# Position scores of an attention stage made evenly over the tiles, 14 tiles ahead

## The reference, cut to what matters

```python
x = L0_attn_w                                     # (2, 2048, 256) float32
x = x + 0.5 * ffn(layernorm(x))                   # 8 experts of rank 16, top 2
x = x + attn(layernorm(x))
x = x + 0.5 * ffn(layernorm(x))

def attn(w):                                      # 16 heads of width 16, 2 sequences
    AC = einsum('bhid,bhjd->bhij', q + u_bias, k)
    BD = einsum('bhid,hjd->bhij', q + v_bias, rp) # rp: (4095 relative positions) @ Wr.T
    BD = rel_shift(BD)                            # row i is moved by i
    return softmax((AC + BD) * 0.25) @ v
```

## Time and profile before

| | us |
|---|---|
| median of 3 runs | 3423.48 (3422.01 to 3426.68) |
| the profiled execution | 3423.38, its span 3421.6 |
| busy in the span: TensorE | 3015.8 (88%) |
| ScalarE | 2591.6 (76%) |
| VectorE | 2486.6 (73%) |
| POOL | 2404.1 (70%) |
| mean granted clock of TensorE | 0.944 |

### The profile page before, as it was taken

One profiled execution on the slowest core, in us unless ns is written; L12 is line 12 of the kernel. 1 busy time (PEld: TensorE's weight loads), 2 busy tenths in 40 slices (PEclk: granted clock), 3 DMA queues, 4 the chain that ended last, 5 costly groups with the idle time before them and its releaser, 6 DMA issues. The chain is left out here.

```text
span 3421.6 us, 112672 instructions
## 1 busy us (share of the span) xinstructions
PE 3015.8 (88%) x40768; PEld 2061.1 (60%) x40768; DVE 2486.6 (73%) x4784; ACT 2591.6 (76%) x4106; POOL 2404.1 (70%) x4104
## 2 busy tenths in 40 slices
PE   4556399999999999998999999999999999989965
PEld 2444066666666666666666666666666666666645
DVE  2555177777787878787878787877787787878866
ACT  2334388888888878787888888887888888878832
POOL 3223687777788878786878877877877887868820
PEclk8778599999999999999999999999999999999987
DMA  5232799999999999999999989999999999999951
GB/s 188 92 104 97 185 202 208 201 201 204 199 210 208 212 198 211 199 212 191 207 217 208 216 198 205 208 205 198 215 206 207 208 210 211 206 198 206 209 155 50
DMA packets 326603, 655.70 MB, mean 192 GB/s; under 512 B 191536, under 2 KB 283568, under 8 KB 292784
## 3 DMA queue, kind: packets, MB, share of 16 engines
q0 software_dynamic: 190464, 524.79, 72.4%
q1 hardware_dynamic: 135600, 123.75, 14.8%
HBM read 77.48 MB, written 46.14 MB: 36 GB/s over the span
## 5 line engine op out<-in xcount | busy, mean ns | idle before, releaser
L653 POOL DMA_DIRECT2D score<-score x3968 | 2272.5, 576 | 632.8 <-ACT score L894 568.9
L892 ACT COPY score<-pos_bank 128x512 f32<-128x512 f32 x2048 | 1087.9, 608 | 439.1 <-PE pos_bank L768 434.3
L902 ACT ACTIVATE score<-score,low 128x1024 f32<-128x1024 f32 x1024 | 1211.3, 1184 | 17.5 <-DVE low L953 11.7
L835 PE MATMUL pt_bank<-ident_sb,score 128*128 128x128 f32 x8192 | 1121.5, 278 | 29.5 <-issue 20.6
L835 PEld LDWEIGHTS pt_bank<-ident_sb,score 128*128 128x128 f32 x8192 | 954.5, 142 | 317.3 <-DVE prob_t L962 78.7
L953 DVE CUSTOM_DVE_ANT_0 score<-ac_bank,score 128x1024 f32<-128x1024 f32 x512 | 627.0, 1225 | 571.0 <-PE ac_bank L821 526.2
L962 DVE COPY prob_t<-pt_bank 128x512 f32<-128x512 f32 x1536 | 1008.6, 684 | 10.0 <-PE pt_bank L835 9.1
L953 DVE CUSTOM_DVE_ANT_0 score<-ac_bank,score,low 128x1024 f32<-128x1024 f32 x512 | 656.5, 1282 | 115.4 <-PE ac_bank L821 95.9
L768 PE MATMUL pos_bank<-pos,qv 96*32 96x512 bf16 (+15 forms) x12160 | 635.6, 318 | 80.8 <-DMA qv<-qv_parts 53.8
L849 PE MATMUL acc_bank<-prob_t,vs 128*32 128x128 f32 x16384 | 678.2, 281 | 29.8 <-issue 29.5
L821 PE MATMUL ac_bank<-ks,qu 96*128 96x512 bf16 x2048 | 628.8, 389 | 13.0 <-issue 7.1
(11 more groups left out here) (94 smaller groups left out, 935.9 us busy)
## 6 DMA issues: line engine op xcount, KB each, us to landing
score<-score POOLq DMA_DIRECT2D x3968, 129.0 KB, 6.5
pos<-pos_parts SPq DMA_DIRECT2D x96, 128.0 KB, 9.3
ks<-k_parts SPq DMA_DIRECT2D x192, 64.0 KB, 7.5
qu<-qu_parts SPq DMA_DIRECT2D x768, 16.0 KB, 7.8
qv<-qv_parts SPq DMA_DIRECT2D x576, 16.5 KB, 6.9
v_heads<-v_sb SPq DMA_DIRECT2D x8, 1024.0 KB, 7.3
vs<-v_heads SPq DMA_DIRECT2D x32, 256.0 KB, 9.0
pos_parts<-part SPq DMA_DIRECT2D x16, 384.0 KB, 2.7
```

The source lines that it names most:

```text
L653: pool.dma_start(pairs_of_tiles(score[s::QUAD, at:at + FT, :], 0), pairs_of_tiles(score[s::QUAD, at:at + FT, :], QUAD - 1 - s))\
L835: last = pe.matmul(PT[c % 2][:, t * P:(t + 1) * P], lhsT=score[:, slot(k), c * BANK + t * P:c * BANK + (t + 1) * P], rhs=ident_sb[:, :], i ...
L892: act.copy(score[:, at + f, c * BANK:(c + 1) * BANK], ring(m)[:, :]).then_inc(pos_out, 1)
L902: act.activation(cols, cols, ACT.Exp, bias=low[:, slot(k), NH - 1:NH], scale=-1.0)\
```

## The change

Three things change together, and the counts of the waits with them.
- The 17 items of a group are spread as 4, 4, 4 and 5 over its four tiles (`MADE_OF`), and `made_at` picks them by (k + POS_AHEAD) % 4, so that each body makes the items of the tile k + POS_AHEAD, two in each half (2 and 3 for the last of a group).
- `POS_AHEAD` is 14 in place of 11. The items of a group are thus made at k % 4 = 2, 3, 0, 1. Before the first content 14 tiles of positions are made, not 12. ScalarE's take of a tile waits for the slot's old tile alone to be turned (two bodies before), not for its whole group.
- `FOLD_AT` is 4 (bank 1), and the fold is made at k % 4 = 2, `finish` at k % 4 = 3, each one tile later. The load of `qv` is issued at k % 4 = 1, and five groups of it stand ahead of the loop.

```diff
--- before.py
+++ after.py
@@ -539,7 +539,7 @@
             NT = 12 * NI
             FIRST, STEPS = 4, 2
             PAIR = NB * NI
-            POS_AHEAD, AC_AHEAD = 11, 2
+            POS_AHEAD, AC_AHEAD = 14, 2
             GQ = FT * P
             QVW = GQ + 16
             PSL = 4
@@ -617,8 +617,8 @@
             def slot(k):
                 return k % (RING * FT)
 
-            MADE_AT = (range(0), range(0, 6), range(6, 12), range(12, ITEMS))
-            FOLD_AT = MADE_AT[1].stop
+            MADE_OF = (range(0, 4), range(4, 8), range(8, 12), range(12, ITEMS))
+            FOLD_AT = MADE_OF[0].stop
             ACT_COPIES = ((1, 3), (), (3,), (3,))
             COPIES = [(k, c) for k in range(FT) for c in range(NK)]
             BY_ACT = [(k, c) for k, c in COPIES if c in ACT_COPIES[k]]
@@ -626,7 +626,7 @@
 
             def fold_no(k):
 
-                return (k - FT - 1) // FT
+                return (k - FT - 2) // FT
 
             def ring(m):
 
@@ -634,7 +634,7 @@
 
             def made_at(k, h):
 
-                items = MADE_AT[k % FT]
+                items = MADE_OF[(k + POS_AHEAD) % FT]
                 middle = (items.start + items.stop) // 2
                 return range(items.start, middle) if h == 0 else range(middle, items.stop)
 
@@ -710,7 +710,7 @@
 
                 def body(step, k):
                     j = (k + POS_AHEAD + 5) // FT
-                    if k % FT == 0 and group_there(step, j):
+                    if k % FT == 1 and group_there(step, j):
                         positions_made(step, k + POS_AHEAD)
                         load_qv(step, j)
                     pair = k // PAIR + 1
@@ -746,7 +746,7 @@
                 load_vs(0, 0)
                 load_qu(0, 1)
                 load_ks(0, 1, range(len(K_PARTS)))
-                for j in (2, 3):
+                for j in (2, 3, 4):
                     positions_made(0, FT * (j - 1) - 1)
                     load_qv(0, j)
                 tile_steps(sp, body, 4)
@@ -864,19 +864,19 @@
                         if there(step, n):
                             for m in made_at(k, h):
                                 positions(step, n // FT, m)
-                        if h and k % FT == 1 and group_there(step, fold_no(k)):
+                        if h and k % FT == 2 and group_there(step, fold_no(k)):
                             fold(step, k)
                         if there(step, k + AC_AHEAD + h):
                             content(step, k + AC_AHEAD + h, 1 - h)
 
-                for j in range((POS_AHEAD + 1) // FT):
-                    for m in range(ITEMS):
-                        positions(0, j, m)
+                for n in range(POS_AHEAD):
+                    for m in MADE_OF[n % FT]:
+                        positions(0, n // FT, m)
                 for k in range(AC_AHEAD):
                     for h in range(NH):
                         content(0, k, h)
                 content(0, AC_AHEAD, 0)
-                tile_steps(pe, body, 2)
+                tile_steps(pe, body, 3)
 
             @block.scalar
             def _(act):
@@ -884,10 +884,10 @@
 
                 def take(step, j, m):
 
-                    if m == 0 and group_there(step, j - RING):
-                        act.wait_ge(turned, tile(step, (j - RING + 1) * FT) * NK)
+                    at, f, c = j % RING * FT, m // NK, m % NK
+                    if c == 0 and f < FT and group_there(step, j - RING):
+                        act.wait_ge(turned, tile(step, (j - RING) * FT + f + 1) * NK)
                     act.wait_ge(pos_full, group(step, j) * ITEMS + (m + 1))
-                    at, f, c = j % RING * FT, m // NK, m % NK
                     if m < ITEMS - 1:
                         act.copy(score[:, at + f, c * BANK:(c + 1) * BANK], ring(m)[:, :]).then_inc(pos_out, 1)
                     else:
@@ -932,9 +932,9 @@
                             exponential(step, k + 1, 1)
                         if h == 0 and there(step, k) and NK - 1 in ACT_COPIES[k % FT]:
                             copy(step, k, NK - 1)
-                for j in range((POS_AHEAD + 1) // FT):
-                    for m in range(ITEMS):
-                        take(0, j, m)
+                for n in range(POS_AHEAD):
+                    for m in MADE_OF[n % FT]:
+                        take(0, n // FT, m)
                 for h in range(NH):
                     exponential(0, 0, h)
                 tile_steps(act, body, 1)
@@ -963,7 +963,7 @@
 
                 def finish(step, k):
 
-                    j, h = (k - FT - 2) // FT, (k - FT - 2) // NI
+                    j, h = (k - FT - 3) // FT, (k - FT - 3) // NI
                     dve.wait_ge(fin_full, group(step, j) + 2)
                     fin = POS[FOLD_AT % 3][:, 0:FT * VW].rearrange("p (f w) -> p f w", w=VW)
                     dve.reciprocal(rden[:, :], fin[:, :, DH]).then_inc(inverted, 1)
@@ -978,7 +978,7 @@
                     n = k + AC_AHEAD
                     if there(step, n):
                         add(step, n, 0)
-                    if k % FT == 2 and group_there(step, (k - FT - 2) // FT):
+                    if k % FT == 3 and group_there(step, fold_no(k)):
                         finish(step, k)
                     for h in range(NH):
                         if h and there(step, n):
@@ -989,7 +989,7 @@
                 for k in range(AC_AHEAD):
                     for h in range(NH):
                         add(0, k, h)
-                tile_steps(dve, body, 3)
+                tile_steps(dve, body, 4)
 
 
         with ExitStack() as c3:

```

## The result

The changed kernel is slower: 3642.03 us (median of 4 runs, 3635.59 to 3664.45) against 3425.08 us, ratio 1.0642 with a 95% interval of 1.0591 to 1.0693, or +217 us. The forecast was slower, but 3466 us; the measured time lies far above its range (3380 to 3525 us).

A forecast was written before the change was run, and what follows sets the result against it. TensorE leads, but the others are so close that order decides: the chain inside a group of four tiles, plus some 153 us of disturbances. 51 + 5.5 - 2 - 12 = +42.5 on 3423.5 gives 3466 us, range 3380 to 3525.

The forecast's parts named there:

- The fold's wait goes: TensorE's fold no longer waits for ScalarE to empty its bank: 0.31 us saved each, 33.2 us over 119 folds before.
- ScalarE's queue in t0: At k % 4 = 0 two takes delay ScalarE's bank 1 copy; the tile takes 5.80 in place of 4.42 us.
- The other tiles: Tiles k % 4 = 1, 2, 3 (t1, t2, t3) were worked out at 4.95, 5.75 and 5.23 us.
- 51 us of chain and 3.5 at start and end: Attention stage: +0.41 us a group over 124.5 groups, +51; +5.5 in front of the stage, -2 at its end.
- The clock: TensorE's granted clock, 1.00 in an undisturbed group, was not expected to fall from the new 0.96 us gap.
- The loads on SP: SP's later qv and qu loads have about 21 us until use, land in under 10, and so cost nothing.
- -12 us for disturbed groups: In about 30 groups slowed by late instructions ScalarE's chain doesn't set the pace, so their +0.41 us each is dropped.
- The rivals: Late instructions rarer 0.12, t0's copy not binding 0.08, no difference 0.06, more late instructions 0.09, clock falls 0.03.
- The fallen clock: TensorE's clock falls after the new gap, one half per group slowed: +1 us a group, +125, 3590 us; chance 0.03.
- More late instructions: Loads of positions and keys meet another phase of the moves; a quarter more of 153 us, +38, 3504 us; chance 0.09.

The follow-up runs named there:

- e11: The changed kernel with a third buffer for qu, its load issued one group earlier against its use: 3494.58 us, ratio 1.0171.
- e4: The kernel before with only SP's part of the change, qv issued at the end of body k % 4 = 1 with qu behind it: 3665.28 us, ratio 1.0746.
- e2: The changed kernel with ScalarE's copy of piece 1 ahead of the takes at k % 4 = 0: 3613.25 us, ratio 1.0570.
- e9: The changed kernel with ScalarE's copy ahead of the takes and three buffers each for qv and qu: 3457.05 us, ratio 1.0096.
- e10: The kernel before with 27 of the 31 moves of a group, four left out: 3360.91 us, ratio 0.9788.

## Why the prediction was right and where it was wrong

- *The fold's wait goes.* Right: 33.2 us before, 1.8 after.
- *ScalarE's queue in t0.* Right, step by step: copy at 3.11 (3.12), t1's turn at 5.82 (5.80), group 21.75 (21.73). The other tiles too: 4.94, 5.75 and 5.24 us for t1, t2 and t3 in the group from 2456.90 us (4.95, 5.75, 5.23). The wait stands in the list with 94.9 us in 126 instructions, about one a group.
- *51 us of chain and 3.5 at start and end.* Mechanism right, and the size nearly: 0.43 us x 124.5 is 54 us by the undisturbed groups, and the first sums_out comes 3.7 us later. The pair without moves differs by 66 us.
- *The clock.* Right that a gap of 0.76 us costs nothing: 1.00 in the undisturbed stretch. It did fall behind the longer waits for qu, which had no place in my sum. The Trainium skill's warning (TensorE: Matmul & The Clock Gate, A second HAM failure mode) doesn't show for short gaps here.
- *The loads on SP: "four tiles, about 21 us, until use and land in under 10: nothing".* **This step failed.** It compared the time to land with the time to use and left out what SP needs to issue them. The row stood in the earlier trace rows: 1392/1610/1828 ns for one issue. Twelve of those are 19 us, plus 8 to land: 27 us, against four tiles of 21 to 22. The runs show 24.2 us in the median from qv's first issue to qu's landing against 21.5, and 184.3 us of waits for qu. I used that very row for the start of the stage and not for the loop. The third qu buffer takes 147 us back (e11) and leaves 69 to the kernel before, about the 66 us by which the order of the engines differs without moves. That these two nearly make 217 is no proof of the split: SP's part alone costs 248 us on the kernel before (e4), and the copy ahead of the takes gives only 29 while qu is late (e2).
- *-12 us for disturbed groups.* Wrong in kind. I took late instructions as a fixed sum of 153 us. They aren't: 90 us of waits for issue before, 19 in the changed kernel (DMA share 0.88), 115 with the third qv buffer (0.96), 150 in e9 (0.97), and nearly none without moves (0.13). The share alone doesn't set them, for e10 has 59 us at 0.84.
- *The rivals.* None came true. The fallen clock was nearest in time (3590 us), and for the wrong reason: the clock stays at 1.00 across the new gap and falls behind waits for qu, and TensorE's own instructions take 33.7 us more, not 125. "More late instructions" (3504 us) goes the other way, since the waits for issue fell. No rival named a late load, for the step above had priced it at nothing.

## What to carry to other kernels

When a load is moved, follow its queue: sum the issue times of all that stands ahead of it, at the duration that the trace shows under load, add the landing, and compare with the distance to its use; a wait put in front of one load delays all that are issued behind it. A queue that issues for 18 of 22.5 us (SP before the change) is nearly a resource at its limit, though its engine shows no busy time, and the place of a load in it then counts. And what is cheap to issue can still land late: look at the landing as well. And where the DMA engines are at 0.97, a faster chain of compute engines buys little: relieve the transfers first.

## What the runs showed of the hardware

- SP's issue of a 16 KB load takes 0.37 us in the median with one move a group. With 31 it takes 1.49 and 1.63 us (kernel before, changed kernel) if it starts while POOL issues moves, and 0.47 and 0.41 us in the pause between them.
- Three DMAs of 48, 32 and 16 KB in place of six of 16 KB issue in a quarter of SP's time and report 23 landings in place of 96. A load of qu takes 23.7 us in place of 16.6 from first issue to last landing in the changed kernel (+56 us, 3642 to 3698). In the kernel before (+240 us) no load of queries is waited for, and VectorE waits for late moves.
- Waits for issue on TensorE grow with the traffic of the DMA engines, but not by their share alone: 90 us at 0.97 and 150 in e9 at the same share, 59 at 0.84, 19 at 0.88 in the changed kernel, under 10 at 0.13, the ends of the loop among them.
- Right behind a wait of 7.18 us eight transposes take 1.92 us in place of 1.04; in an undisturbed group with its wait of 0.76 us the granted clock stays at 1.00.
